# Gated cross-attention and quantized MLP on one core: probabilities turned by DMA instead of TensorE, weight jobs re-slotted, half of the gated magnitudes taken a stage earlier

## The chip, the cores and the metric

One core of one Trainium2 chip. The metric is device microseconds of one execution. In the text PE is TensorE, PEld its weight load, DVE VectorE, ACT ScalarE, POOL GpSimd, SP SyncE; "SPq" is SP's queue of DMA issues. SP computes nothing: it issues nearly all transfers, in program order, and a wait in it holds everything behind.

## What is computed

The input x is 4 batches of 1024 rows by 512; the context has 64 rows per batch. 16 heads of 64.

```python
x = x + tanh(g_xattn) * attention(layernorm(x), ctx)   # softmax over 64 keys, causal mask; @ w_o
x = x + tanh(g_ffn) * ffn(layernorm(x))
# ffn, with q() = fake quantization to 16 bits by the largest magnitude of the whole tensor:
up, gate = q(x @ deq(w_up).T), q(x @ deq(w_gate).T)     # 1536 columns
f = q(gate * round16(sigmoid(gate)))
out = q(f * up) @ deq(w_down).T
# deq(): 4-bit weights, a scale for every block of 32
```

Each q() needs a maximum over all 4096 rows before the first value can be quantized, which is why the program has stages with a hard border between them.

## The kernel before

Every product that matters is made of f16 parts, high and low: a = ah + al, b = bh + bl, and ah·bh + ah·bl + al·bh, three matmuls with 512 columns. Five stages follow each other, with a barrier of all engines at each border.

1. **Front** (`front_phase`): weights of attention are loaded and multiplied into per-batch matrices A (queries times keys) and V (values times w_o), then attention runs over 32 tiles of 128 rows, in steps. `schedule` calls on each engine a `step(b, k, ...)`; in step k the work of several tiles is done, each at another point of its life: layernorm of tile k+2, scores of tile k, softmax of tile k−1, values of tile k−2, second layernorm and output of tile k−3. The loop runs over eight steps, one batch (counted here as steps 3 to 10, and by k modulo 8).
   - PE, step k: 8 transposes (L1096) of the probabilities `pr` (f32, 128 by 1024) of tile k−2 into PSUM `pT`; 24 matmuls of scores (L1072); 24 of values (L1043). In steps 0 and 1 the next batch's A (`keys`, L1009) and V (`four_heads`, L1023) are made in between, and ACT and DVE split them in parts.
   - ACT and DVE split the turned probabilities from PSUM: `pTh` (L690), `pTl` (L906), in two halves each. DVE then subtracts the row maximum (L804, L808), ACT takes exp (L714), DVE sums (L839) and takes the reciprocal (L842), POOL multiplies (L652, `prob_done`).
   - SP, step k: stores x1 and x2, loads the next x, turns `nh`, `nl` of tile k+2 by DMA (L582).
   - **Jobs** (class `Jobs`): each dequantizes 128 by 512 of a weight: load, `job_scale` (DVE), `job_divide` (POOL), multiply back (DVE, `deq_done`), `hi` (ACT), `lo` (POOL or DVE), turn, store. In attention there are four a batch for w_gate, with two sets of buffers (`JB = 4`, NJ = 2), and SP turns them by DMA (L597).
2. **Gate** (`gate_phase`): 96 products of 12 matmuls (L1414), 24 in each round of its loop; ACT evicts (L1304), DVE takes extremes, SP spills to `gate_d`. Six jobs a round prepare w_up (first half, turned by DMA, L1246) and w_down (second half, turned by PE in `job_turn`, L334, and stored straight from `hi` and `lo`, L361).
3. **Up** (`up_phase`): 96 products. Beside it, for each of 32 tiles of 1536 columns, ACT takes the sigmoid of the gate (L1555); in the first half DVE searches the largest gated value (`lowest`), in the second (`slot_of(k)` gives tile k its product, k from 32) DVE computes f = gate · sigmoid · scale into `nq` as int16 (`gated`, L1603). A fresh product's maximum costs DVE one more operation (L1643).
4. **Magnitudes** (first half of `down_phase`): max |f · up| over everything. Per tile ACT makes |up| as integers (L1820) and |f| (L1826), DVE multiplies and reduces (L1850). For every third tile, `signed(k)`, ACT leaves |f| out and DVE makes two passes, with either sign. PE has nothing to do but `keep_warm`.
5. **Down**: quantize f · up (L1903), split it, 96 times 12 matmuls (L1937), `finish` adds x1, output.

The waits around the change, in the code's words:

```python
def signed(k):                                    # magnitudes, before
    return k == 0 or k % 3 == 2
if have(k - 2):                                   # PE's step, before
    pe.wait_ge(*tile(prob_done, b, j))
    ...
        mm = pe.transpose(pT[:, p * P:(p + 1) * P], pr[j % 2][:, p * P:(p + 1) * P], ident[:, :])
```

## Time and profile before

| | us |
|---|---|
| runs before: median (lowest to highest) | 1346.55 (1345.92 to 1348.36) |
| the profiled execution, its own time | 1344.37 |
| its span, first to last instruction | 1342.5 |
| front: first matmul of attention's scores / last of values, start | 50.7 / 481.8 |
| gate: first / last product matmul, start | 492.0 / 745.9 |
| up: first / last product matmul, start | 751.3 / 999.8 |
| magnitudes: first / last reduction, start | 1006.1 / 1083.7 |
| down: first product matmul, start | 1088.8 |

How to read what follows: a row of a timeline has the start, the length, the engine, the line of the kernel, the operation, what it writes and reads, how many instructions are merged, and in brackets how long the engine sat idle before and who released it. Matmuls are pipelined: one of 512 columns shows as 0.38 us, but the next starts 0.216 us later. A row of windows has the stretch, then for each engine its busy time and count, the granted clock of TensorE as a share of 2.4 GHz, the DMA engines' share and GB/s.

### The profile page before, as it was taken

The numbers are of one execution on the slowest core, as the hardware profiler recorded it, in microseconds if no ns is written. First come the engines' busy times: TensorE is split into PE (matmuls) and PEld (weight loads), VectorE is DVE, ScalarE is ACT, GpSimd is POOL, SyncE is SP. The second block draws the span as 40 slices with busy tenths as digits, with TensorE's granted clock in tenths as the row PEclk, the third lists the DMA queues.
The fourth block names the chain that finished last, engine by engine and source line by source line (L and its number), as shares of the span: only waits on it lengthen the run. The fifth ranks groups of instructions, "written<-read, shape, count | busy, mean of one in ns | idle before, by whom it ended". The sixth has DMA issues, their size and how long they took to land. (4 is left out here: it accounts for less than half of the span.)

```text
span 1342.5 us, 18904 instructions
## 1 busy us (share of the span) xinstructions
PE 1218.1 (91%) x5937; PEld 593.9 (44%) x5937; DVE 1001.7 (75%) x1444; ACT 672.2 (50%) x782; POOL 291.6 (22%) x375
## 2 busy tenths in 40 slices
PE   7899899999899989999999999999980079999998
PEld 6644544544444444444444444444430034444443
DVE  2778789779777667777777699979999975555554
ACT  3534444444353334444443588857669963343341
POOL 0246435535534221111111222300210000000000
PEclk9999999999999999999999999999995589999999
DMA  9123523533434458787876899943389854454453
GB/s 333 35 53 106 140 84 84 140 94 98 124 91 130 139 195 227 239 257 233 244 214 205 292 329 339 328 140 132 133 274 340 300 181 142 164 182 162 163 176 106
DMA packets 187403, 246.64 MB, mean 184 GB/s; under 512 B 99280, under 2 KB 111568, under 8 KB 187344
## 3 DMA queue, kind: packets, MB, share of 16 engines
q1 hardware_dynamic: 187056, 245.95, 57.0%
q8 instruction: 25, 0.41, 0.1%
q14 instruction: 34, 0.28, 0.1%
q10 hardware_dynamic: 288, 0.00, 0.0%
HBM read 136.32 MB, written 91.23 MB: 169 GB/s over the span
## 5 line engine op out<-in xcount | busy, mean ns | idle before, releaser
L1414 PE MATMUL gpG<-xph,Wh 128*128 128x512 f16 x384 | 145.6, 379 | 1.4 <-DVE xpl L1329 1.4
L1937 PE MATMUL pD<-Wh,xph 128*128 128x512 f16 x384 | 145.5, 379 | 1.0 <-DVE xpl L1912 1.0
L1414 PE MATMUL gpG<-xpl,Wh 128*128 128x512 f16 x384 | 145.5, 379 | 0.0
L1414 PE MATMUL gpG<-xph,Wl 128*128 128x512 f16 x384 | 145.5, 379 | 0.0
L1414 PE MATMUL pU<-xph,Wh 128*128 128x512 f16 x384 | 145.5, 379 | 0.0
L1414 PE MATMUL pU<-xpl,Wh 128*128 128x512 f16 x384 | 145.5, 379 | 0.0
L1414 PE MATMUL pU<-xph,Wl 128*128 128x512 f16 x384 | 145.5, 379 | 0.0
L1937 PE MATMUL pD<-Wl,xph 128*128 128x512 f16 x384 | 145.5, 379 | 0.0
L1937 PE MATMUL pD<-Wh,xpl 128*128 128x512 f16 x384 | 145.5, 379 | 0.0
L1304 ACT ACTIVATE gst<-gpG,rw 128x512 f32<-128x512 f32 x96 | 65.7, 685 | 130.9 <-PE gpG L1414 103.2
L1342 DVE TENSOR_REDUCE gmx<-gst 128x512 f32 (+1 forms) x96 | 65.4, 682 | 56.6 <-ACT gst L1304 56.4
L1072 PE MATMUL pS<-Ah,xh 128*128 128x512 f16 x256 | 76.2, 379 | 4.1 <-DVE Vl L783 4.1
L1555 ACT ACTIVATE gb<-nq,sc 128x1536 f32<-128x1536 int16 x48 | 75.3, 1568 | 4.6 <-POOL nq L1535 4.4
L1428 PE MATMUL pD<-ident 128*128 128x512 f16 x28 | 7.8, 440 | 75.6 <-DVE pmx L1850 75.6
L1072 PE MATMUL pS<-Ah,xl 128*128 128x512 f16 x256 | 76.1, 379 | 0.0
L1072 PE MATMUL pS<-Al,xh 128*128 128x512 f16 x256 | 76.1, 379 | 0.0
L652 POOL TENSOR_TENSOR pr<-pr,srec 128x1024 f32<-128x1024 f32 x32 | 60.8, 1901 | 68.2 <-DVE srec L842 67.8
L1569 ACT ACTIVATE ust<-pU,rw 128x512 f32<-128x512 f32 x72 | 49.0, 683 | 45.4 <-PE pU L1414 40.1
L690 ACT ACTIVATE pTh<-pT 128x512 f16<-128x512 f32 x64 | 34.7, 595 | 68.3 <-PE pT L1096 68.2
L714 ACT ACTIVATE pr<-pr,fit 128x1024 f32<-128x1024 f32 x32 | 36.7, 1148 | 62.9 <-DVE pr L808 44.1
L313 POOL TENSOR_TENSOR gjw<-gjw,gjinv 128x512 f32<-128x512 f32 x24 | 25.2, 1049 | 190.4 <-DVE gjinv L301 190.4
L1343 DVE TENSOR_REDUCE gmx<-gst 128x512 f32 (+1 forms) x96 | 64.8, 675 | 0.0
(248 smaller groups left out, 2615.5 us busy)
## 6 DMA issues: line engine op xcount, KB each, us to landing
dub<-up_d SPq DMA_DIRECT2D x42, 768.0 KB, 4.7
gate_d<-gst SPq DMA_DIRECT2D x96, 256.0 KB, 3.2
gb<-gate_d SPq DMA_DIRECT2D x24, 768.0 KB, 6.9
up_d<-ust SPq DMA_DIRECT2D x72, 256.0 KB, 5.0
eu<-up_d SPq DMA_DIRECT2D x22, 768.0 KB, 6.6
xr<-xn_d SPq DMA_DIRECT2D x9, 1024.0 KB, 6.4
xin<-in_x SPq DMA_DIRECT2D x32, 256.0 KB, 3.6
x_d<-x SPq DMA_DIRECT2D x32, 256.0 KB, 2.3
```

The lines of the kernel that those rows point to most:

```text
L313: pool.tensor_tensor(blocks(J.w[n][:, :]), blocks(J.w[n][:, :]), spread(J.inv[:, n, :]), ALU.mult).then_inc(J.div_done, 1)
L652: pool.tensor_tensor(p3, p3, srec[:, j % 2, :].unsqueeze(2).to_broadcast([P, HEADS, CK]), ALU.mult).then_inc(prob_done, 1)
L690: act.activation(pTh[:, cs], pT[:, cs], ACT.Copy, scale=P_TOP).then_inc(pTh_done, 1)
L714: act.activation(pr[j % 2][:, :], pr[j % 2][:, :], ACT.Exp, scale=S_UNIT).then_inc(exp_done, 1)
L1072: mm = pe.matmul(pS[k % 2][:, hf * 512:(hf + 1) * 512], xs[k % 4][:, cs], As[:, kt, hf * 512:(hf + 1) * 512], start=(kt == 0 and xs is xh ...
L1304: act.activation(stage[n][:, :], pG[m % 3][:, :], ACT.Copy, scale=row_scale[0][:, it:it + 1]).then_inc(g_sb, 1)
L1342: dve.tensor_reduce(gmx[:, 1, bass.ds(2 * IT * i + m, 1)], stage[m % NS][:, :], X, ALU.min).then_inc(g_neg, 1)
L1343: dve.tensor_reduce(gmx[:, 0, bass.ds(2 * IT * i + m, 1)], stage[m % NS][:, :], X, ALU.max).then_inc(g_pos, 1)
L1414: mm = pe.matmul(ps[:, :], Ws[:, it, kt * P:(kt + 1) * P], xs[:, kt, :], start=(kt == 0 and Ws is Wh and xs is xh), stop=(kt == KT - 1 and ...
L1555: act.activation(gb[k % NG][:, :], nq[:, k % QT, :], ACT.Sigmoid, scale=S_G).then_inc(sig_done, 1)
L1569: act.activation(stage[n][:, :], pU[m % NU][:, :], ACT.Copy, scale=scale[:, it:it + 1]).then_inc(u_sb, 1)
L1937: mm = pe.matmul(pD[4 * t + q][:, :], os_[n][:, cs], Ws[:, it, :], start=(it == 0 and os_ is oh and Ws is Wh), stop=(it == IT - 1 and os_ ...
```

## The change

- **Attention.** The probabilities are split before they are turned: ACT writes `p_high`, DVE `p_low`, each 128 by 1024 in one instruction, from SBUF. SP turns each in two halves by DMA (four DMA transposes a tile) into one of two buffers `pTh`, `pTl`. PE's transposes and PSUM's part in it are gone; PE multiplies the values of tile k−3 in step k, so second layernorm and output move to tile k−4, and there is one step more (k to BQ+3). V is made in step 2 instead of 1.
- **Jobs in attention** have four sets of buffers and one slot more to the end: `lo` moves behind POOL's probabilities and `job_divide`, `hi` to the start of ACT's step, `deq` behind DVE's sums.
- **Gate.** w_down's jobs are turned by DMA like w_up's; their stores come one job later, and the last one's waits at the end of the stage's queue for its turn.
- **Up, magnitudes, down.** For every second tile (`AWAY`), DVE's `gated` writes into a staging buffer `f_away`; ACT writes |f| into `nq`, SP spills f to `f_d`. Magnitudes need no |f| for these tiles; of the others every fourth is `signed`. Down loads f of these tiles again (`load_f`).

```diff
@@ front_phase, SP's step
+                if have(k - 2):
+                    j = k - 2
+                    sp.wait_ge(*tile(pl_done, b, j))
+                    sp.sem_inc(J.apart, 1)
+                    sp.wait_ge(*tile(o_ps, b, j - 2))
+                    sp.sem_inc(J.apart, 1)
+                    for part_, to in ((p_high, pTh), (p_low, pTl)):
+                        for cs in halves:
+                            sp.dma_start_transpose(blocks_of(to[j % 2][:, cs]), part_[:, cs]).then_inc(pt_in[j % 2], 16)
-                j = k - 3
+                j = k - 4
...
@@ front_phase, POOL's step (job_divide stays ahead of it)
-                    pool.tensor_tensor(J.lo[n][:, :], J.d[n][:, :], J.hi[n][:, :], ALU.subtract).then_inc(J.lo_done, 1)
...
+                    pool.tensor_tensor(J.lo[q][:, :], J.d[q][:, :], J.hi[q % 2][:, :], ALU.subtract).then_inc(J.lo_done, 1)
@@ front_phase, ACT's step
-                    act.wait_ge(*tile(o_ps, b, j - 1))
-                    for h, cs in enumerate(halves):
-                        act.wait_ge(*part(pT_ps, b, j, h))
-                        act.activation(pTh[:, cs], pT[:, cs], ACT.Copy, scale=P_TOP).then_inc(pTh_done, 1)
+                    act.wait_ge(*tile(prob_done, b, j))
+                    act.wait_ge(*p_turned(b, j - 1))
+                    act.activation(p_high[:, :], pr[j % 2][:, :], ACT.Copy, scale=P_TOP).then_inc(ph_done, 1)
@@ front_phase, DVE's step
+                        dve.wait_ge(*tile(ph_done, b, j))
+                        dve.scalar_tensor_tensor(out=p_low[:, :], in0=pr[j % 2][:, :], scalar=P_TOP, in1=p_high[:, :],
+                                                 op0=ALU.mult, op1=ALU.subtract).then_inc(pl_done, 1)
@@ front_phase, PE's values and step
-                j = k - 2
+                j = k - 3
                 if have(j):
+                    pe.wait_ge(*p_turned(b, j))
...
-                    for p in range(PAIRS):
-                        mm = pe.transpose(pT[:, p * P:(p + 1) * P], pr[j % 2][:, p * P:(p + 1) * P], ident[:, :])
@@ gate_phase, end of SP's round
+            turned_store(sp, i, JR - 1, job_dst(i, JR - 1))
@@ gate_phase, PE
-                        if it % 4 == 3 and t:
-                            job_turn(pe, J, i, 3 * t + it // 4, ident)
@@ up_phase
+        away = {(m // IT, m % IT): [k for k in range(QT, 2 * QT) if k - QT in AWAY and slot_of(k) + 3 == m] for m in range(FT * IT)}
...
+                    for k in away[j, it]:
+                        sp.wait_ge(f_done, k + 1)
+                        sp.dma_start(f_d[AWAY.index(k - QT), :, :], f_away).then_inc(f_out, 16)
...
+                    for k in away[j, it]:
+                        act.wait_ge(f_done, k + 1)
+                        act.activation(nq[:, k - QT, :], f_away, ACT.Abs).then_inc(f_abs, 1)
...
+                if k - QT in AWAY:
+                    to, n = f_away, AWAY.index(k - QT)
+                    if n:
+                        dve.wait_ge(f_abs, n)
+                        dve.wait_ge(f_out, 16 * n)
@@ down_phase
+            stay = [k for k, g in enumerate(ORDER) if g not in AWAY]
...
-                return k == 0 or k % 3 == 2
+                return k in stay and stay.index(k) % 4 == 0
```

Three places of the order of instructions. First SP's queue in one step of attention with a job's store and turn (k = 7 before, k = 9 of the change). `pTh`, `pTl` are the turned probabilities, `xh`, `xl` the turned layernorm, `pjhiT` the turned job, `x_d`, `xn_d` the outputs. Before:

```order
L558 DMA x_d<-x 128x512
L561 ISA
L561 DMA xin<-in_x 128x512
L563 DMA xn_d<-x 128x512
L577 REGISTER_ALU
L582 DMA_TRANSPOSE xh<-nh 128x4x128
L582 DMA_TRANSPOSE xl<-nl 128x4x128
L589 ISA
L589 DMA wgate_hi<-pjhiT 128x512
L589 DMA wgate_lo<-pjloT 128x512
L597 DMA_TRANSPOSE pjhiT<-pjhi 128x4x128
L597 DMA_TRANSPOSE pjloT<-pjlo 128x4x128
```

and of the change:

```order
L568 DMA_TRANSPOSE pTh<-p_high 128x4x128 x2
L568 DMA_TRANSPOSE pTl<-p_low 128x4x128 x2
L573 ISA
L573 DMA x_d<-x 128x512
L576 ISA
L576 DMA xin<-in_x 128x512
L578 DMA xn_d<-x 128x512
L592 REGISTER_ALU
L597 DMA_TRANSPOSE xh<-nh 128x4x128
L597 DMA_TRANSPOSE xl<-nl 128x4x128
L604 ISA
L604 DMA wgate_hi<-pjhiT 128x512
```

Four DMA transposes now stand at the head of each step's issues, ahead of the two of the layernorm and the job's two. Second, POOL in a step with a job's `lo`: `pjlo` is the job's low part, `pr` the probabilities, `pjw` the job's division, `nl` the low part of the next tile's layernorm. Before:

```order
L645 ISA [waits pj_hi]
L646 TENSOR_TENSOR pjlo<-pjd,pjhi 128x512 [waits pj_turn_in0]
L652 TENSOR_TENSOR pr<-pr,srec 128x1024 [waits rec]
L312 REGISTER_ALU
L313 TENSOR_TENSOR pjw<-pjw,pjinv 128x512 [waits pj_inv]
L317 TENSOR_SCALAR pjq<-pjw 128x512 [waits pj_div,pj_deq]
L661 TENSOR_TENSOR nl<-xn,nh 128x512 [waits xt_in1,xh]
```

and of the change:

```order
L661 TENSOR_TENSOR pr<-pr,srec 128x1024 [waits rec]
L315 REGISTER_ALU
L316 TENSOR_TENSOR pjw<-pjw,pjinv 128x512 [waits pj_inv]
L320 TENSOR_SCALAR pjq<-pjw 128x512 [waits pj_div,pj_deq]
L669 ISA [waits pj_hi]
L670 TENSOR_TENSOR pjlo<-pjd,pjhi 128x512 [waits pj_turn_in0]
L674 REGISTER_ALU [waits xh]
L675 TENSOR_TENSOR nl<-xn,nh 128x512 [waits xt_in0]
```

The job's `lo`, which waits for ACT and for a DMA transpose, has moved from ahead of the probabilities to behind them. Third, the end of SP's queue in the gate stage, of the change (before, the last rows are the two stores of `gjhi` and `gjlo` without the transposes ahead):

```order
L1201 DMA gate_d<-gst 128x512 x2
L1246 DMA wdown_hi<-gjhiT 128x4x128
L1246 DMA wdown_lo<-gjloT 128x4x128
L1235 DMA_TRANSPOSE gjhiT<-gjhi 128x4x128
L1235 DMA_TRANSPOSE gjloT<-gjlo 128x4x128
L1246 DMA wdown_hi<-gjhiT 128x4x128
L1246 DMA wdown_lo<-gjloT 128x4x128
L1151 UNCONDITIONAL_BRANCH
```

The last job is turned and then stored behind everything else, in front of the stage's border.

## Rows read from the trace of the kernel before

**Rows 1.** The page: span and share of each engine.
```profile
PE 1218.1 (91%) x5937; PEld 593.9 (44%) x5937; DVE 1001.7 (75%) x1444; ACT 672.2 (50%) x782; POOL 291.6 (22%) x375
```

**Rows 2.** Windows of attention: us, busy (x instructions) of five engines, clock, DMA, GB/s.
```profile
178.45:287.90 109.45, 102.76 (x548) 52.58 (x544) 87.81 (x149) 48.61 (x71) 52.78 (x77) 1.00 0.38 106
...
396.87:481.39 84.52, 80.51 (x402) 39.26 (x398) 58.80 (x87) 29.75 (x42) 30.25 (x48) 1.00 0.46 134
```

**Rows 3.** Timeline of PE in attention: start us, us, instruction, idle before it.
```profile
214.39 1.09 PE L1096 MATMUL pT<-ident,pr 128*128 128x128 f32 x8 [0.64 <-POOL pr L652]
215.32 0.59 PE L1072 MATMUL pS<-Ah,xh 128*128 128x512 f16 x2
...
220.50 0.38 PE L1043 MATMUL pX<-Vh,pTh 128*128 128x512 f16 x1
...
253.51 1.09 PE L1096 MATMUL pT<-ident,pr 128*128 128x128 f32 x8 [2.74 <-POOL pr L652]
...
272.18 1.04 PE L1096 MATMUL pT<-ident,pr 128*128 128x128 f32 x8
...
461.36 0.59 PE L1072 MATMUL pS<-Ah,xl 128*128 128x512 f16 x2
...
481.82 0.38 PE L1043 MATMUL pX<-Vh,pTl 128*128 128x512 f16 x1
```

**Rows 4.** Timeline of DVE, one step of attention with a job.
```profile
215.95 0.68 DVE L846 TENSOR_REDUCE xmx<-x 128x1 f32<-128x512 f32 x1
...
224.83 0.63 DVE L283 TENSOR_REDUCE pjmx<-pjw 128x16 f32<-128x512 f32 x1
...
227.58 0.67 DVE L846 TENSOR_REDUCE xmx<-x 128x1 f32<-128x512 f32 x1
```

**Rows 5.** Groups by line, POOL and ACT in attention: busy, mean ns, idle before.
```profile
L652 POOL TENSOR_TENSOR pr<-pr,srec 128x1024 f32<-128x1024 f32 x32 | 60.8, 1901 | 68.2 <-DVE srec L842 67.8
...
L661 POOL TENSOR_TENSOR nl<-xn,nh 128x512 f16<-128x512 f32 x32 | 37.0, 1157 | 23.4 <-ACT nh L678 23.4
...
L690 ACT ACTIVATE pTh<-pT 128x512 f16<-128x512 f32 x64 | 34.7, 595 | 68.3 <-PE pT L1096 68.2 <-issue 0.2
```

**Rows 6.** One line of SP's queue (min/median/max ns), and its landing.
```profile
L582 SPq DMA_TRANSPOSE xl<-nl x32: 1239/1253/2307, 40.5 to 446.6; - x32
...
DMA to landing us min/median/max: 2.4/2.5/4.2
```

**Rows 7.** Timeline at one gate job's turn, and at the gate's end.
```profile
533.88 0.60 PE L334 MATMUL gjbank<-ident,gjd 128*128 128x128 f32 x4
534.31 0.38 PE L1414 MATMUL gpG<-xph,Wh 128*128 128x512 f16 x1
...
749.13 0.51 SPq L361 DMA_DIRECT2D wdown_lo<-gjlo  x1
...
750.59 0.40 PE L1421 MATMUL upR<-ident,sc 128*128 128x128 f32 x2 [1.52 <-PEq L1157]
```

**Rows 8.** The up stage's second half: a window, DVE's gating, landing of a store.
```profile
905.00:930.00 25.00, 25.00 (x117) 11.37 (x116) 25.00 (x23) 16.50 (x17) 2.26 (x2) 1.00 0.43 148
...
L1603 DVE SCALAR_TENSOR_TENSOR nq<-nq,sc,mb x16: 1802/1811/2971, 897.9 to 998.4; 128x1536 int16<-128x1536 int16 x16
...
up_d<-ust SPq DMA_DIRECT2D x72, 256.0 KB, 5.0
```

**Rows 9.** The magnitude stage: timeline at its start, in it and at its end; a window.
```profile
1006.07 1.82 DVE L1850 CUSTOM_DVE_ANT_0 xfa<-nq,dui,pmx 128x1536 int16<-128x1536 int16 x1 [0.22 <-DVE nq L1695]
...
1022.83 1.48 ACT L1826 ACTIVATE last_m<-nq 128x1536 int16<-128x1536 int16 x1
...
1030.21 1.48 ACT L1826 ACTIVATE xfa<-nq 128x1536 int16<-128x1536 int16 x1
...
1010.00:1020.00 10.00, 0.00 (x0) 0.00 (x0) 9.74 (x11) 8.73 (x7) 0.00 (x0) 0.50 0.97 377
...
1085.43 0.08 DVE L1850 DVE_READ_ACCUMULATOR2_ANT pmx<- 128x1 f32 x1
```

More of the change, by code:

```diff
@@ L402, in front_phase @@
         pr = [sb(ph, f"pr{n}", [P, INNER], F32) for n in range(2)]
-        pTh = sb(ph, "pTh", [P, INNER], F16)
-        pTl = sb(ph, "pTl", [P, INNER], F16)
+        p_high = sb(ph, "p_high", [P, INNER], F16)
+        p_low = sb(ph, "p_low", [P, INNER], F16)
         x1 = [sb(ph, f"x1{n}", [P, H], F32) for n in range(2)]
@@ L438, in front_phase @@
         Vl = sb(ph, "Vl", [P, PAIRS, H], F16)
+        pTh = [sb(ph, f"pTh{n}", [P, INNER], F16) for n in range(2)]
+        pTl = [sb(ph, f"pTl{n}", [P, INNER], F16) for n in range(2)]
         pw = [pS[0][:, 0:512], pS[0][:, 512:1024]]
@@ L452, in front_phase @@
                o_ps x1 stats2 mean2 eps2 rstd2 x2 x2max""".split())
-        pT_ps, pTh_done, pTl_done = (sem(n, 16) for n in ("pT_ps", "pTh", "pTl"))
+        ph_done, pl_done = (sem(n, 8) for n in ("ph", "pl"))
+        pt_in = [sem(f"pt_in{n}", 64) for n in range(2)]
         kbd_set, vb_set = sem("kbd_set"), sem("vb_set")
@@ L465, in schedule @@
         def schedule(eng, step, straight=False):
-            for k in range(-2, 3):
+            for k in range(-2, 4):
                 step(0, k, lambda j: j >= 0, False)
@@ L470, in schedule @@
                 for b in range(B - 1):
-                    for k in range(3, BQ + 3):
+                    for k in range(4, BQ + 4):
                         step(b, k, lambda j: True, True)
@@ L708, in step @@
                     normal(b, j, xn, xin[j % BQ], mv, rs, xn_done)
+                q = job_at(k, jobs, 2)
+                if q is not None:
+                    act.wait_ge(*at(J.deq_done, JB * b, q + 1))
+                    act.wait_ge(*at(turn_in[q % 2], 16 * JB * b, 32 * (q // 2)))
+                    act.activation(J.hi[q % 2][:, :], J.d[q][:, :], ACT.Copy).then_inc(J.hi_done, 1)
                 def exponentials():
@@ L972, in step @@
                     fit_v()
[L973 to L974 removed]
+                if have(k - 4):
+                    largest(b, k - 4)
             for r in range(2):
@@ L1048, in values @@
                     if which == 0 and p < PAIRS - 1:
-                        if p == 2 and have(j):
-                            pe.wait_ge(*part(pTl_done, b, j, 1))
                         keys(b, k, ahead, p + 1)
@@ L1166, in gate_phase @@
         AHEAD = 5
-        J = Jobs(mk, ph, "gj", JR, NJ, [pb(ph, "gjbank")])
-        turned = [[sb(ph, f"gj{part}T{n}", [P, 512], F16) for part in ("hi", "lo")] for n in range(3)]
-        turn_in = [sem(f"gj_turn_in{n}", 32) for n in range(3)]
+        J = Jobs(mk, ph, "gj", JR, NJ, None)
+        turned = [[sb(ph, f"gj{part}T{n}", [P, 512], F16) for part in ("hi", "lo")] for n in range(JR)]
+        turn_in = [sem(f"gj_turn_in{n}", 32) for n in range(JR)]
         pG = [pb(ph, f"gpG{n}") for n in range(3)]
@@ L1784, in _, with load_f @@
                     sp.dma_start(xub[k % NB], up_d[g, :, :]).then_inc(xu_in[k % NB], 16)
+                def load_f(g):
+                    n = AWAY.index(g)
+                    if n < 2:
+                        sp.wait_ge(xui_done, [k for k in range(QT) if k % NB == 2 + n][-1] + 1)
+                    else:
+                        sp.wait_ge(o_done, AWAY[n - 2] + 4)
+                    sp.dma_start(fr[n % 2], f_d[n, :, :]).then_inc(fr_in[n % 2], 16)
+                sp.wait_ge(f_out, 16 * len(AWAY))
+                for g in AWAY[0:2]:
+                    load_f(g)
                 for g in range(2):
```

235 lines of the change are left out of this document (115 added, 120 removed).

## The prediction

> **What bounds the kernel now.** I read the page first: PE is busy for 91% of the span and DVE for 75% [rows 1], so the question is where PE is not the limit. The stages answer it. Gate, up and down are 1152 matmuls each at a pitch of 0.216 us, 248.8 us, and by the table they take hardly more. Two places are left. **Attention**: the windows over whole batches [rows 2] show 109.45 us a batch with PE busy 102.8, DVE 87.8. In PE's timeline [rows 3] a step starts with the eight transposes, and what PE waits for there is POOL's multiplication `pr` (0.64, 2.74 us). **Magnitudes**: 1006.1 to 1085.5 us, PE idle, DVE and ACT both near full, DMA share up to 0.97 [rows 9]. A gain must come from these, or from work taken off PE.
>
> **Attention, PE's side.** The transposes cost 0.93 us a step (214.39 to 215.32), scores 5.18, values again 5.18 (24 at 0.216) [rows 3]. A plain step needs 11.3 us before, 10.4 after. The step with A takes 18.67 us (253.51 to 272.18), the next, with V, 15.72 (to 287.90, end of the window): after, 17.7 and 14.8. A batch of the change is then 6 x 10.36 + 17.7 + 14.8 = 94.7 us of PE, 14.7 less than it takes now. That is the floor, if everyone else keeps up.
>
> **Attention, the others.** DVE's step with a job is 11.63 us without a gap (215.95 to 227.58), 2.75 of it the job's scale (from 224.83) [rows 4]. DVE's new `low` is one instruction of 1024 instead of two of 512, about 1.2 us as now. Over a batch I get 94.7 for DVE too: step 4 about 11.0, three of 11.63, steps 0 and 2 about 14.5, three plain ones of 9.9. In a plain step the circle is reciprocal, POOL 1.90, ACT's `p_high` 1.1 (two of 0.595 [rows 5], less overlap), `low`, subtraction, exp, sums: 9.9 us, under PE's.
> The new resource is SP's queue. A DMA transpose is issued for 1.25 us and lands 2.5 after its start [rows 6], so four take 4.9 us and 1.3 more to land. ACT may write `p_high` again only when they have landed. This closes a chain over two steps: `nl` done, two transposes of it (2.5), next step's four (6.2), `p_high` 1.1, `low` 1.2, DVE up to the reciprocal 5.6 (its step [rows 4] without job, `low` and first statistics), POOL's `pr` 1.9 and `nl` 1.2 [rows 5], with waits between 20.1 us, 10.0 a step. Without jobs PE stays the bound, barely. With jobs the chain of the even steps takes in 7.8 us of SP (two turns of 2.5, stores, loads), 6.1 of POOL (division and `lo`, operations of `nl`'s size, now ahead of `nl`), 1.2 of DVE and some 7 of parts of A and V: 80.2 + 22.1 = 102.3 us a batch. That is above both floors. I take 102.5; bounds 95 (the floor) and 109.5 (no idle gained).
>
> Terms, attention:
> - three batches at 102.5 instead of 109.3: -20.4;
> - the last batch's four plain steps and scores, 52.3 us now (409.55 to 461.8), 4 x 10.36 + 5.18 = 46.6 after: -5.7;
> - the start: the values of the first tile leave step 2, so step 3 starts 0.93 + 5.18 earlier: -6.1, paid back at
> - the end: the last scores to the last values take 461.8 to 482.0, 20.2 us [rows 3]. Of the change: subtraction 2.5, then `p_high` of the last tile must wait until the tile before has landed (its `low` at 4.4, 6.2 to land: 10.6), 1.1, 1.2, 6.2, values 5.2 = 24.3: +4.1.
> Sum -28.1, bounds from -51 (94.9 a batch) to -8 (109).
>
> **Gate.** A turn of four transposes costs 0.43 us (533.88 to 534.31) [rows 7], 12 of them 5.2 us. But the stage ends by SP: its last issue ends at 749.64, and all engines go on at 750.5 [rows 7]. Now the last job is turned first: two issues 2.5 and a landing 1.3 more, 3.8 us. Net -1.4 (bounds -5.2, +1).
>
> **Up.** DVE is busy 25.00 of 25 us in the second half [rows 8]: it has no room. ACT gets 16 magnitudes of 1.48 us over 106 us and has 8.5 of 25 free, so it carries them. The staging buffer is one: tile n+2 may be gated when f of tile n is in memory, and SP issues that three products after its slot. Slots of such tiles are 2 or 3 products (2.59 us each) apart. The first time DVE is ready at about 903.5 us and the spill lands at 906.7 (issue 902.7; landing 2 to 5, the latter the row of the smaller spill [rows 8]); later DVE's lag hides it. A full DVE can't win the lag back: +2.5 (bounds 0, +12, twice 16 waits of 0.4).
>
> **Magnitudes.** Now 43 passes in 79.4 us, 1.85 each; ACT's five operations per three tiles take 7.38 us (1022.83 to 1030.21), 1.48 each, so the two engines are equally full [rows 9]. After: DVE 32 + 4 = 36 passes, ACT 32 + 12 = 44 operations: 36 x 1.83 = 65.9 and 44 x 1.48 = 65.1 us: -13.4. A tile is 768 KB every 2.06 us, 382 GB/s; the window at 0.97 share shows 377 [rows 9]. Six buffers and four early loads cover most of it: +1 (bounds 0, +5). `keep_warm` starts a shorter time ahead: +0.4. Sum -12.0.
>
> **Down** gets 16 loads of 384 KB, issued a tile ahead, under PE's 245 us: 0. Nothing else moves there.
>
> **Sum**: -28.1 - 1.4 + 2.5 - 12.0 = -39.0. The profiled execution took 1344.4 us (span 1342.5 and 1.9 around it), so 1305.4 on it; the median of the runs is 2.2 above, and 1346.6 - 39 = **1307.6 us**, 2.9% less.
>
> **Rivals.**
> - *PE's floor is reached* (SP runs ahead where steps 0 and 2 are long, and DVE's lag is elastic by most of a step): 94.9 a batch, 23 us less than forecast: 1285. For it: both floors are equal, and only the chain through SP is longer; its extras may overlap better than I add them. Against: two engines at their floor at once is rare. 0.17.
> - *VectorE and GpSimd get in each other's way*, or the chain through SP is longer: 107.5 a batch: +15, with +3 in up: 1325. For it: DVE's gating shows 2971 ns beside a median of 1811 [rows 8], with POOL at work then; `low` now reads both operands from SBUF, and POOL's `nl` or division may run beside it. Against: `nl` mostly ends where `low` starts. By the Trainium skill (GPSIMD Engine Reference, 1. Specifications) the two share their SBUF interfaces when DVE has two SBUF inputs; this case's slow instance agrees. 0.23.
> - *SP's queue becomes the bound, slower than before.* A transposing DMA of the six to eight in a row takes longer than 1.25 us: the row has one at 2307 ns, and a landing of 4.2 [rows 6]. SP's step is six transposes and 1.0 of plain issues, in four steps a batch two transposes and 1.3 more. At 1.2 us each that is 83 us a batch; at 1.8, 8 x 11.8 + 4 x 4.9 = 114; three batches +14, last batch +2, end +6, less 11 from the rest: 1358. It decides from 1.7 us a transpose. Against: 64 issues of this kind in this attention keep to the median, though never more than four in a row. 0.05.
>   The Trainium skill (VectorE: DVE Perf Modes, The three transpose paths and Rules for kernel authors) says to turn 128 by 128 on TensorE if PSUM will do, 390 ns against 1309 by DMA. As an estimate by that page, 16 blocks a tile would be 21 us of DMA a step if they ran one by one, twice PE's step. The row disagrees: four blocks are issued in 1.25 us and there in 2.5.
> - *Only magnitudes gain*: the probabilities' turn is late in every step (a wait of PE on `pt_in` takes the place of the one on POOL): 109 a batch, 1327 to 1340. 0.05; the rest is scattered.
>
> **Chances.** Forecast 0.50 (1297 to 1316), floor 0.17, contention 0.23, queue 0.05, late turn 0.05. The range from **1285 to 1330** leaves out the queue, half of the late turn and the lower part of the floor. A change of 0.2%, 2.7 us, is about what can be told from none. Faster 0.94, within 0.01, slower 0.05.
>
> **What would show it.** Attention: PE's L1072 to L1052 without transposes; a batch 102.5 us; PE's wait on a landing of `pTh`/`pTl` in the step with A, ACT's `p_high` waiting for a DMA in steps 7 to 3, not in plain ones; transposes at 1.2 us each. Last scores to last values 24 us. Gate: products 248.8 without gap, barrier 3 us after the last product is reduced. Up: one wait of DVE on the spill at the first tiles, end 2 to 3 us later. Magnitudes 66 us, DMA share above 0.95. Wrong: a batch under 97 or over 107, DVE waiting for the spill again and again, ACT waiting for loads in magnitudes.

## The result, and the profile after

The changed kernel takes **1363.84 us** (median of 4 runs, 1362.95 to 1365.2), the kernel before in the same session 1346.24 (1344.47 to 1348.36): ratio 1.0131, 95% interval 1.0113 to 1.0149. It is 1.3% slower; 1307.6 was forecast, 1285 to 1330. The profiled execution took 1362.95 us, span 1361.1, 18.6 above the span before. The page's head and its row of the clock:

```profile
span 1361.1 us, 18490 instructions
PE 1206.1 (89%) x5633; PEld 568.2 (42%) x5633; DVE 992.9 (73%) x1398; ACT 674.9 (50%) x757; POOL 307.9 (23%) x375
...
PEclk9979899899899989999999899999996579999999
```

PE has 12 us less to do than before [rows 1], so the loss is waiting. Two bounds of its terms were broken as well: a batch had 109.5 us as its upper bound ("no idle gained") and took up to 113.3, and the gate had +1 and got +7.8. The stages, cut at PE's instructions in both timelines (us, after minus before):

| stretch | before | after | difference | forecast |
|---|---|---|---|---|
| to the first batch's scores of tile 3 (the first behind V in the change, the second before) | 82.60 | 80.94 | -1.7 | -6.1 |
| three batches | 327.8 | 335.0 | +7.2 | -20.4 |
| last batch, to the end of its last scores | 51.4 | 48.3 | -3.1 | -5.7 |
| last scores to last values | 20.2 | 33.2 | +13.0 | +4.1 |
| gate, from the last values to the first product of up | 269.2 | 277.0 | +7.8 | -1.4 |
| products of up | 248.9 | 251.0 | +2.1 | 0 |
| last product of up to the turn of its maximum | 2.1 | 9.3 | +7.1 | +2.5 |
| from there to the first product of down | 86.5 | 72.7 | -13.8 | -12.0 |
| rest | 253.7 | 253.7 | 0 | 0 |

**Attention.** PE's timeline around the step with A of the second batch, and the scores behind V at the two ends of that batch (start, us, engine, line, operation, what it waited for):

```profile
189.83 0.60 PE L1078 MATMUL pS<-Ah,xh 128*128 128x512 f16 x2 [2.23 <-DVE Vl L796]
...
239.62 0.39 PE L1052 MATMUL pO<-Vh,pTh 128*128 128x512 f16 x1 [0.76 <-DMA pTl<-p_low]
...
254.18 2.07 PE L1019 MATMUL pS<-kbd,wqT 128*128 128x128 f32 x8 [9.21 <-DMA pTl<-p_low]
256.04 0.63 PE L1052 MATMUL pX<-Vh,pTh 128*128 128x512 f16 x1
...
302.60 0.61 PE L1078 MATMUL pS<-Ah,xh 128*128 128x512 f16 x2 [2.23 <-DVE Vl L796]
```

The batch takes 302.60 - 189.83 = 112.8 us (the three: 108.9, 112.8, 113.3), while plain steps take the 10.36 forecast. Most of what is lost stands in one place: at the step with A, where values come first in the step, PE waits 9.21 us for the tile's low part to land (5.96 and 8.21 in the other batches). Who waits in attention, by the waits of PE, ACT and SP (60 to 500 us):

```profile
PE pS L1019 <- DMA pTl<-p_low: 23.4, 3, 9.2
PE pS L1078 <- DVE Vl L796: 9.0, 4, 2.3
PE pO L1052 <- DMA pTl<-p_low: 7.5, 3, 6.0
...
ACT p_high L703 <- DMA pTl<-p_low: 55.7, 19, 5.5
...
SPq L593 <- POOL nl L675: 52.5, 23, 9.9
...
SPq L563 <- DVE p_low L917: 10.1, 4, 3.9
```

A row of waits has the total in us, the number of times and the longest. The last two rows are the telling ones: SP waits for `p_low` four times only. It stands at the wait for `nl` (23 times, 52.5 us), in front of the probabilities' turns of the next step. One step with a job on GpSimd and on SP's queue:

```profile
236.16 2.23 POOL L661 TENSOR_TENSOR pr<-pr,srec 128x1024 f32<-128x1024 f32 x1
238.79 1.05 POOL L316 TENSOR_TENSOR pjw<-pjw,pjinv 128x512 f32<-128x512 f32 x1 [0.40 <-DVE pjinv L290]
...
241.76 2.13 POOL L675 TENSOR_TENSOR nl<-xn,nh 128x512 f16<-128x512 f32 x1
```

```profile
244.06 1.21 SPq L597 DMA_TRANSPOSE xh<-nh  x1
245.31 1.25 SPq L597 DMA_TRANSPOSE xl<-nl  x1
246.90 0.35 SPq L250 DMA_DIRECT2D pjw<-in_L_ffn_w_gate  x1
247.50 2.50 SPq L568 DMA_TRANSPOSE pTh<-p_high  x2
250.06 2.57 SPq L568 DMA_TRANSPOSE pTl<-p_low  x2
```

And VectorE in the same step, which has no gap of more than 0.17 us in it:

```profile
235.82 0.25 DVE L854 RECIPROCAL srec<-ssum 128x16 f32<-128x16 f32 x1
...
237.26 1.16 DVE L288 TENSOR_SCALAR pjs<-pjmx 128x16 f32<-128x16 f32 x1
...
241.55 1.33 DVE L917 SCALAR_TENSOR_TENSOR p_low<-pr,p_high 128x1024 f16<-128x1024 f32 x1
```

`p_low` ended at 242.88; its turns started at 247.50 and the last landed at 253.9. VectorE's step is long too: from one `p_low` to the next 12.30 us (229.25 to 241.55), where a step with a job took 11.63 before [rows 4] and PE now needs 10.36. One part of that is `L288`, an operation on 16 columns, 1.16 us here and 0.32 at 225.50 in the timeline of before; in the mean of attention's 12 it takes 1267 ns, 842 before. Not every step is like this one: in the four steps with jobs of this batch VectorE takes 50.3 us from `p_low` to `p_low` (204.71 to 255.04), in the other four, with A and V among them, 62.5 (191.23 to 204.71 and 255.04 to 304.01):

```profile
191.23 1.19 DVE L917 SCALAR_TENSOR_TENSOR p_low<-pr,p_high 128x1024 f16<-128x1024 f32 x1
...
204.71 1.23 DVE L917 SCALAR_TENSOR_TENSOR p_low<-pr,p_high 128x1024 f16<-128x1024 f32 x1 [4.28 <-ACT p_high L703]
...
255.04 2.10 DVE L917 SCALAR_TENSOR_TENSOR p_low<-pr,p_high 128x1024 f16<-128x1024 f32 x1 [0.55 <-ACT p_high L703]
...
304.01 1.19 DVE L917 SCALAR_TENSOR_TENSOR p_low<-pr,p_high 128x1024 f16<-128x1024 f32 x1
```

**The end of attention, and the stages behind.** PE's timeline at the last values, at the end of gate, of up and of magnitudes:

```profile
471.97 0.39 PE L1052 MATMUL pX<-Vh,pTh 128*128 128x512 f16 x1 [2.39 <-DMA pTl<-p_low]
...
483.28 0.61 PE L1052 MATMUL pO<-Vh,pTh 128*128 128x512 f16 x1 [5.95 <-DMA pTl<-p_low]
...
492.19 0.39 PE L1052 MATMUL pX<-Vh,pTh 128*128 128x512 f16 x1 [0.98 <-DMA pTl<-p_low]
...
507.66 0.61 PE L1405 MATMUL gpG<-xph,Wh 128*128 128x512 f16 x1 [0.89 <-DVE xpl L1324]
...
764.43 2.75 PE L1419 MATMUL gpX<-ident 128*128 128x512 f16 x12
773.09 0.66 PE L1412 MATMUL upR<-ident,sc 128*128 128x128 f32 x2 [5.91 <-PEq L1151]
...
1034.68 0.48 PE L1412 MATMUL upR<-ident,sc 128*128 128x128 f32 x1 [9.26 <-DVE sc L1661]
...
1097.24 7.28 PE L1419 MATMUL pD<-ident 128*128 128x512 f16 x20 [62.09 <-DVE pmx L1881]
```

At 1097.24 is the gain: PE waits 62.09 us for VectorE's 36 passes of 1.81 us, 75.6 before for 43. At 1034.68 is what it cost: up ends with VectorE 9.26 us behind (2.1 before), since it waited for the spill of `f`, five times and not once. ScalarE's wait for a spill of gate's products more than doubled. The same waits before, then of the change:

```profile
PE pD L1428 <- DVE pmx L1850: 75.6, 1, 75.6
...
ACT gst L1304 <- DMA gate_d<-gst: 24.7, 10, 3.5
...
PE upR L1421 <- DVE sc L1651: 2.1, 1, 2.1
```

```profile
DVE x_rows L1613 <- DMA f_d<-x_rows: 9.7, 5, 3.0
...
ACT gst L1304 <- DMA gate_d<-gst: 58.3, 15, 6.7
```

### The profile page after: what moved, and what is told of

The parts are those of the page before. It is cut to its first block and busy times, and to the rows that moved or that the text cites. A ratio compares the mean times of both kernels' runs of the same rounds, so it can differ in the third digit from the quotient of the medians.

```text
span 1361.1 us, 18490 instructions
## 1 busy us (share of the span) xinstructions
PE 1206.1 (89%) x5633; PEld 568.2 (42%) x5633; DVE 992.9 (73%) x1398; ACT 674.9 (50%) x757; POOL 307.9 (23%) x375
## 5 line engine op out<-in xcount | busy, mean ns | idle before, releaser
L1078 PE MATMUL pS<-Ah,xh 128*128 128x512 f16 x256 | 77.6, 385 | 13.9 <-DVE Vl L796 9.0
L661 POOL TENSOR_TENSOR pr<-pr,srec 128x1024 f32<-128x1024 f32 x32 | 63.8, 1993 | 78.1 <-DVE srec L854 77.3
L703 ACT ACTIVATE p_high<-pr 128x1024 f16<-128x1024 f32 x32 | 33.8, 1055 | 70.6 <-DMA pTl<-p_low 55.7
L917 DVE SCALAR_TENSOR_TENSOR p_low<-pr,p_high 128x1024 f16<-128x1024 f32 x32 | 42.3, 1323 | 36.1 <-ACT p_high L703 35.9
L686 ACT ACTIVATE xn<-xin,rs 128x512 f32<-128x512 f32 x32 | 26.0, 812 | 83.0 <-POOL rs L649 83.0
```

Of the source, the lines that this page charges most:

```text
L661: pool.tensor_tensor(p3, p3, srec[:, j % 2, :].unsqueeze(2).to_broadcast([P, HEADS, CK]), ALU.mult).then_inc(prob_done, 1)
L686: act.activation(to[n][:, :], src[:, :], ACT.Identity, bias=rs_[:, n, 2:3], scale=rs_[:, n, 1:2]).then_inc(done, 1)
L703: act.activation(p_high[:, :], pr[j % 2][:, :], ACT.Copy, scale=P_TOP).then_inc(ph_done, 1)
L917: dve.scalar_tensor_tensor(out=p_low[:, :], in0=pr[j % 2][:, :], scalar=P_TOP, in1=p_high[:, :], op0=ALU.mult, op1=ALU.subtract).then_inc( ...
L1078: mm = pe.matmul(pS[k % 2][:, hf * 512:(hf + 1) * 512], xs[k % 4][:, cs], As[:, kt, hf * 512:(hf + 1) * 512], start=(kt == 0 and xs is xh ...
```

## The experiments

Each time is a median, with the ratio to the kernel before on the same chip and its interval. A batch runs from the scores behind V to those of the next. The kernel before has medians from 1346.1 to 1349.0 us in these sessions, so differences between two experiments are given from their traces where a few us matter.

### The three parts alone

**only_attention**: of the diff only what stands in `front_phase` and the jobs' class.

> The kernel before with the change's attention alone (probabilities turned by DMA, values a step later, jobs reordered); gate, up, magnitudes and down are those of before. By the prediction on record attention gives 28.1 us: 1318. By the trace of the whole change attention lost 15.5 us (last values end at 497.4 us and not at 482.0) and nothing behind it belongs to it: 1362, the last values again near 497. A rival: the gate and up lose time because attention leaves DMA or the clock in another state; then this kernel comes out slower than 1364, with a gate of more than 254 us.

1363.05 us, 1.0099 (1.0075 to 1.0123). Batches 109.2, 112.6, 113.3; the last values end at 500.5 (482.0 before, 497.4 in the whole change). The same waits, 23.0 us of them in the three steps with A. Up takes 248.9, and 5.0 us pass from gate's last product to up. Theory held: the attention part alone loses in its batches what the whole does (335.1 us for the three, 335.0 there), 1.7 us more behind them (83.2 us to the last values and not 81.5), and nothing of gate's end.

**only_gate**: of the diff only what stands in `gate_phase`.

> The kernel before with the change's gate alone (w_down's weights turned by DMA, the last store behind the last turn). Prediction on record: -1.4, 1345. Theory from the trace: products 256.4 us and not 253.8 in spite of 12 turns less, of which 2.4 is the first products at the low clock, and 10.2 and not 5.4 us from the last product to the first of up, then 2.2 us of up's first products at 1.2 GHz since PE idled 5.9 us: if these belong to the gate, +7 to +9.6: 1353 to 1356. Rival: the slow first products follow PE's idle time at the end of attention, not the gate: then the products of the gate take about 254, and the sum is +5 to +7.

1353.98 us, 1.0043 (1.0023 to 1.0063). Products from 493.65 to 749.18, 255.5 and not 253.8, with 12 turns less: ScalarE's waits for a spill hold PE up by 3.4. Behind the longest of these waits the granted clock fell too: 0.73 from 640 to 645, 12 matmuls where 23 fit at the full clock. Then 10.5 us to up's first product (5.4 before), and 1.1 more in up. These three are 7.9 us in the trace; the ratio says 5.8. The first products run at the full clock here (granted 1.00 from 493.6 to 499.0, against 0.50 from 507.6 to 512.4 in the whole change): the rival was right in that, those belong to attention's idle end. The barrier, and the slower spills, are gate's own. With 7.9 in the trace and 5.8 by the ratio the run doesn't decide between the theory's sum (+7 to +9.6) and the rival's (+5 to +7).

**only_magnitudes**: of the diff only what stands in `up_phase` and `down_phase`.

> The kernel before with the early magnitudes alone (up, magnitudes, down of the change). Prediction on record: +2.5 in up, -12.0 in magnitudes: 1336.7. Theory from the trace: -13.8 from the first wide reduction to the first product of down, +7.2 between up's last product and the turn of its maximum (DVE's five waits of 9.7 us in all for the spill of f, in an engine without room): 1339.6. Rival: those waits are longer in the whole change only because other DMA work is late; then DVE is done 2 to 3 us after up's last product, as before, and the kernel takes 1333.

1340.83 us, 0.9958 (0.994 to 0.9976). PE's two waits, at the end of up and of magnitudes:

```profile
PE pD L1431 <- DVE pmx L1893: 62.1, 1, 62.1
PE upR L1424 <- DVE sc L1673: 11.6, 1, 11.6
```

The rival fell: VectorE's waits for the spill are there without the other parts (11.8 us, 5 times). From the turn of up's maximum to the first product of down it wins 14.8 us (86.5 before, 71.7 here), and 9.4 are given back in up. The three ratios multiplied give 1.0099 x 1.0043 x 0.9958 = 1.0100, against 1.0131. With intervals of 0.2% on each, this difference of 0.3% can't be told from none.

### What the staging buffer costs

**only_magnitudes_two**: a second buffer for `f`. It lies where the fourth of down's early loads would go; that load is issued behind the last spill instead.

```diff
-        f_out, f_abs = sem("u_f_out"), sem("u_f_abs")
+        f_out, f_abs = [sem(f"u_f_out{n}") for n in range(2)], sem("u_f_abs")
+        f_away = [f_away, early_u[3][:, 0:I // 2].bitcast(I16)]
...
-                    to, n = f_away, AWAY.index(k - QT)
-                    if n:
-                        dve.wait_ge(f_abs, n)
-                        dve.wait_ge(f_out, 16 * n)
+                    n = AWAY.index(k - QT)
+                    to = f_away[n % 2]
+                    if n > 1:
+                        dve.wait_ge(f_abs, n - 1)
+                        dve.wait_ge(f_out[n % 2], 16 * (n // 2))
```

> only_magnitudes with two staging buffers for f (the second in the fourth of down's early loads, which comes after the last spill instead), so that VectorE waits for the spill before the last. Theory (the 11.8 us of VectorE's waits on the one buffer, in an engine without room, are the 9.4 us that up ends later): the waits go, up's maximum is turned 2 to 4 us after its last product and not 11.6, magnitudes stay at 62 us: 1331 to 1334, from 1340.8. Rival: the end is late because ScalarE's 16 extra magnitudes (1.48 us each) or VectorE's slower gating (2.42 us in some) fill the engine: then 1337 to 1341. Rival: the fourth load is now late at the start of magnitudes: +1 to +3 us there.

1335.1 us, 0.9921 (0.9904 to 0.9937). No wait of VectorE on a spill is left, and PE waits 3.18 us for up's maximum, not 11.57; in magnitudes it still waits 62.8 us. The theory held: the loss in up was the one buffer, not the extra magnitudes on ScalarE.

### SP's queue, the landing, or VectorE

**nl_before_jobs**: GpSimd's `nl` moved up, right behind `pr`.

```diff
+                if have(k + 2):
+                    ...
+                    pool.tensor_tensor(nl[j % 2][:, :], xn[j % 2][:, :], nh[j % 2][:, :], ALU.subtract).then_inc(xl_done, 1)
                 q = job_at(k, jobs, 0)
                 if q is not None:
                     job_divide(pool, J, b, q, q + 1)
                 q = job_at(k, jobs, 2)
...
-                if have(k + 2):
-                    ...
-                    pool.tensor_tensor(nl[j % 2][:, :], xn[j % 2][:, :], nh[j % 2][:, :], ALU.subtract).then_inc(xl_done, 1)
```

> The whole change, with GpSimd's nl (x's low part) moved ahead of the job's division and low part, right behind pr. Theory A (SP's queue is the chain: it stands at the wait for nl while p_low has long been done; p's four turns start 1.7 to 6.1 us after p_low, at 219.8, 233.2, 247.5, 262.4, 279.8 us): nl ends some 3 us earlier in the steps with jobs, p's turns too, and the wait of 9.2 us in the step with A falls to 2 to 5 us: 4 to 7 us a batch, 1345 to 1352. Theory B (VectorE is the chain: its step with a job takes 12.3 us against PE's 10.36, and it is without a gap from 214 to 247 us): nothing but the place of the wait changes, within 3 us of 1363.8. Rival C: ACT's and VectorE's part of the job comes later and the next step with them: slower by some us.

1356.43 us, 1.0058 (1.0037 to 1.0079). SP's wait for `nl` falls from 52.5 to 36.7 us. Batches 106.5, 111.5, 110.7, so 2.4, 1.3 and 2.6 less; PE's waits in the step with A 1.65, 6.84 and 6.83. Less than theory A said and more than B: SP's wait is a part of the chain, and behind it VectorE is full (its `p_low` at 215.14, 227.94, 240.57, 253.25, without a gap of more than 0.23 us between).

**plain_p_turns**: the four turns of the probabilities become plain copies. It leaves out the turning, so PE multiplies other data; only its time is of use.

```diff
-                            sp.dma_start_transpose(blocks_of(to[j % 2][:, cs]), part_[:, cs]).then_inc(pt_in[j % 2], 16)
+                            sp.dma_start(to[j % 2][:, cs], part_[:, cs]).then_inc(pt_in[j % 2], 16)
```

> The whole change, with the four turning DMAs of a tile's probabilities replaced by four plain copies of the same 128 KB (the probabilities then stand unturned, so the values are those of other data). A plain issue takes SP 0.35 to 0.6 us and not 1.27, so 2.7 to 3.7 us of SP and part of the landing go from every step. Theory A (chain through SP and the landing): the 9.2 us wait of PE in the step with A falls under 3 us, a batch to 104 or less, the end of attention by some 8 us more: 1325 to 1335. Theory B (VectorE's step of 12.3 us with a job): PE's wait stays at 6 us or more, a batch at 109 to 110, only the end gains: 1345 to 1352. Rival: the turns hold up other engines' DMA and SBUF traffic; then VectorE's own instructions get shorter.

1352.38 us, 1.004 (1.0023 to 1.0058). Batches 109.2, 112.0, 111.0, waits in the step with A 3.69, 6.46 and 5.97; the end of attention gains more. SP's issues of the low part, of the whole change and then here (min/median/max ns):

```profile
L568 SPq DMA_TRANSPOSE pTl<-p_low x64: 1188/1267/2040, 71.9 to 489.6; - x64
```

```profile
L568 SPq DMA_DIRECT2D pTl<-p_low x64: 477/601/815, 69.4 to 478.9; - x64
```

That is close to theory B's forecast (1345 to 1352, batches 109 to 110): with half of the turns' issue gone from SP (1.13 and 1.25 us for what took 2.50 and 2.57) the three waits in the steps with A fall by 7.3 us, but the three batches by 2.8 only. The chain passes through SP but is not made of it.

**nl_narrow_max**: on top of nl_before_jobs 0.6 us less of VectorE a step.

```diff
-                dve.tensor_reduce(xmx[:, bass.ds(BQ * b + j, 1)], x2[j % 2][:, :], X, ALU.max,
+                dve.tensor_reduce(xmx[:, bass.ds(BQ * b + j, 1)], x2[j % 2][:, 0:32], X, ALU.max,
```

> nl_before_jobs, and VectorE takes the maximum of x2 over 32 of the 512 columns only (0.1 and not 0.68 us a tile), so the scale of x is that of a part. In nl_before_jobs PE still waits 6.84 us in the step with A and 2.24 before. Theory B (VectorE, with jobs 12.7 us a step, is what is left): its step gets 0.55 us shorter, four to five steps before the wait, so PE's waits fall by 2 to 3 us a batch: 1348 to 1351. Theory A (SP's chain): nothing, 1356.

1349.06 us, 1.0013 (0.9996 to 1.003): 7.4 less than nl_before_jobs. Batches 104.4, 109.2, 108.5, each 2.1 to 2.3 us shorter. The size is theory B's, the place isn't: PE's waits in the step with A stay (1.00, 6.83 and 6.84 us). In the second batch 1.1 us came from the scores' wait for VectorE's `pr` (2.24, then 1.14) and 1.1 from the keys and values of the step with A, which VectorE's `Al` holds up (17.49 us to the scores, then 16.36).

**two_p_and_nl**: on top of nl_before_jobs two buffers for `p_high` and for `p_low`.

```diff
-                    act.wait_ge(*p_turned(b, j - 1))
-                    act.activation(p_high[:, :], pr[j % 2][:, :], ACT.Copy, scale=P_TOP).then_inc(ph_done, 1)
+                    act.wait_ge(*p_turned(b, j - 2))
+                    act.activation(p_high[j % 2], pr[j % 2][:, :], ACT.Copy, scale=P_TOP).then_inc(ph_done, 1)
```

> nl_before_jobs, with two buffers each for p_high and p_low (the second pair lies where up's late stages do), so that ScalarE's p_high waits for the landing of the tile before the last. Theory A: ScalarE's waits for the landing (55.7 us of them in the whole change) were part of the chain; they go, PE's wait in the step with A falls to 2 us or less, the end of attention gains 5 us: 1335 to 1345. Theory B: with nl early VectorE has no gap in the steps with jobs, p_high comes earlier but p_low doesn't; only the last tiles gain, 3 to 6 us: 1350 to 1353.

1344.24 us, 0.9983 (0.997 to 0.9996). PE's waits, the first two rows, and ScalarE's for `p_high`, where no landing is left:

```profile
PE pS L1019 <- DMA pTl<-late_st: 11.3, 3, 5.4
PE pS L1078 <- DVE Vl L796: 9.0, 4, 2.3
...
ACT p_high L703 <- POOL pr L661: 28.5, 16, 3.1
```

Batches 106.5, 107.9, 107.6, and the last stretch of attention 4 us shorter: 10.4 us in the trace up to the last values, 12.2 by the medians. The time is theory A's, the waits of 4.1 and 5.4 us that stay are more than it allowed (2). So there were three causes: `nl` behind the jobs, one buffer held until it has landed, and VectorE's step. Each was taken away on top of the ones before; what each is worth alone, or in another order, was not tried.

### Two engines in each other's way

**scale_late**: on top of two_p_and_nl, the job's scale changes places with the maximum of `x2`.

```diff
-                q = job_at(k, jobs, 0)
-                if q is not None:
-                    job_scale(dve, J, b, q, unit[:, 3 * q + b:3 * q + b + 1])
                 if k == 0:
                     fit_v()
                 if have(k - 4):
                     largest(b, k - 4)
+                q = job_at(k, jobs, 0)
+                if q is not None:
+                    job_scale(dve, J, b, q, unit[:, 3 * q + b:3 * q + b + 1])
```

> two_p_and_nl, with VectorE's scale of the job one instruction later, behind the maximum of x2 (0.68 us). In the whole change the scale's tensor_scalar over 16 columns takes 1267 ns in the mean (842 in the kernel before; 0.18 where GpSimd stands still), always while GpSimd multiplies pr (1.99 us, from 0.1 us behind the reciprocal). Theory C (the two engines get in each other's way there, and VectorE's step with a job is the bound): it falls to 0.3 to 0.7 us, the step to 12 us or less, PE's wait in the step with A by some 2 us in each batch: 1338 to 1341, from 1344.2. Rival: nl now stands behind pr and gets in the way instead: the instruction stays above 1 us, 1344. Rival: the integers of the job come late and GpSimd's chain with them: 1346 or more.

1343.87 us, 0.9984 (0.9974 to 0.9994). VectorE's groups in attention, first of the whole change, then here (busy us, mean ns | idle before):

```profile
L288 DVE TENSOR_SCALAR pjs<-pjmx 128x16 f32<-128x16 f32 x12 | 15.2, 1267 | 0.4
```

```profile
L288 DVE TENSOR_SCALAR pjs<-pjmx 128x16 f32<-128x16 f32 x12 | 8.3, 693 | 0.4
```

The instruction falls by 0.57 us as theory C said, but the time doesn't follow. Where it went shows at the maximum of `x2`, of two_p_and_nl and then here:

```profile
L858 DVE TENSOR_REDUCE xmx<-x 128x1 f32<-128x512 f32 x31 | 20.8, 669 | 9.1 <-ACT x L686 9.1
```

```profile
L858 DVE TENSOR_REDUCE xmx<-x 128x1 f32<-128x512 f32 x31 | 21.0, 677 | 17.9 <-ACT x L686 17.9
```

The maximum now comes earlier and waits for ScalarE's `x2`: 17.9 us in attention and not 9.1. VectorE is 11.8 us less busy (6.9 in `L288`, 3.8 in `L278` behind it, 1.1 in `p_low`), and 8.8 of it came back as this wait. In some steps the engines still meet: a `p_low` takes 1.92 us (235.89) beside GpSimd's `pjlo`, and that step is 12.69 us (223.20 to 235.89). What is left is 0.5 us a batch. Theory C had the instruction right and the path wrong: ScalarE stood next in line.

This is what the Trainium skill says in SBUF — State Buffer (SBUF: two separate sides), on the port pair that VectorE and GpSimd share: whoever starts first holds it for its whole instruction, against VectorE's instructions in a fast mode or with two inputs in SBUF. The trace agrees. In the whole change `L288` starts at 237.26, inside GpSimd's `pr` (236.16, 2.23 us), and ends at 238.42, 0.03 us behind it; `p_low`, with two inputs from SBUF, takes 2.10 us where it starts inside `nl` (255.04, 254.90) and 1.19 at its least.

### The clock

**warm_in_A**: PE works through its wait.

```diff
                 if have(j):
-                    pe.wait_ge(*p_turned(b, j))
                     pe.wait_ge(*tile(x1_done, b, j - 2))
+                    if which == 0:
+                        keep_warm(pe, pOut[j % 2][:, :], ident, 24)
+                    pe.wait_ge(*p_turned(b, j))
```

> The whole change, with 24 matmuls that are thrown away (5.2 us) on PE ahead of its wait for pTl in the step with A, into the bank that the values then start. The granted clock stood at 0.63 in PE's wait of 9.2 us (248.0 to 254.1) and at 0.51 in the 5.9 us behind it, with products of 634 ns and not 379: by the rows some 2.7 us of the step with A. Theory (the clock falls since PE idles): the granted clock stays at 1.00, the step with A is 2.5 to 3 us shorter in three batches, 1355 to 1357. Rival: the wait is over before the filler is (first batch 5.96 us): then up to nothing in that batch. Rival: the clock doesn't follow PE's idling: nothing, 1364, or some us more.

1365.93 us, 1.0128 (1.0099 to 1.0157), no gain. The windows over the wait and over the first part of the step with A, of the whole change and of this kernel (stretch, its length, busy us of PE, PEld, DVE, ACT, POOL, granted clock, DMA share, GB/s):

```profile
248.00:254.10 6.10, 0.00 (x0) 0.00 (x0) 5.40 (x13) 1.16 (x3) 4.43 (x5) 0.63 0.61 146
254.10:260.00 5.90, 5.82 (x22) 4.53 (x23) 5.03 (x8) 2.28 (x3) 2.60 (x4) 0.51 0.52 156
```

```profile
247.00:253.40 6.40, 3.62 (x17) 1.47 (x15) 5.71 (x13) 1.48 (x3) 4.63 (x6) 1.00 0.60 143
253.40:259.30 5.90, 5.85 (x31) 4.82 (x32) 5.04 (x8) 2.25 (x3) 2.60 (x4) 0.71 0.60 156
```

The clock does follow PE's idling: granted 1.00 in the wait and not 0.63, then 0.71 and not 0.51 (2.83 us of idle time were left). But from the first key to the scores it is 15.56 us here and 15.55 there. PE is done with keys and values 1.1 us sooner, and waits that much longer for VectorE's last part of A ahead of the scores (1.34 us for `Al` and not 0.26). The low clock cost nothing here, where PE was not the limit; a stretch with the clock at 1.00 throughout was not tried.

### The best version

**best**: attention of scale_late, gate of before, magnitudes with two buffers.

> Attention of scale_late, the gate of the kernel before, magnitudes with two staging buffers. By the sum of the parts: attention with nl early and two buffers ends near 481 us and with the late scale near 476 (before: 482.0); gate as before (the change's cost 5 to 9 us); up and magnitudes -12 to -14: 1326 to 1332, 1.1 to 1.5% under before. Rival: the parts do not add (the DMA queue at the end of attention, the clock at the start of the gate): 1333 to 1340.

**1330.36 us**, 0.9886 (0.9869 to 0.9902): 1.1% faster than before, 2.5% than the change. The last values end at 479.1 (482.0 before). By the parts one would get 13.9 us (11.0 of only_magnitudes_two, 2.9 in attention) and has 15.8 by the medians: inside the expected 1326 to 1332.

**best_narrow_max**: the narrow maximum on top of best, which leaves out most of that maximum.

> best, and VectorE takes the maximum of x2 over 32 of 512 columns (the scale of x is that of a part): 0.6 us less of VectorE in each of attention's steps, nothing else. In best a batch takes 106.0, 107.4 and 107.05 us against PE's floor, with PE's waits of 2.1, 6.4 and 4.3 us for pTl in the step with A. Theory B (with nl early and two buffers, what is left of the loss is VectorE's step of 12.3 to 12.7 us with a job against PE's 10.36): these waits fall by about 2 us each (four steps of 0.55), 1323 to 1326. Rival A (SP's turns and their landing are what is left): PE's waits and the time stay, 1330.

1321.08 us, 0.9803 (0.9782 to 0.9823). PE's waits in the steps with A fall to 8.8 us in all from 12.8, batches to 104.2, 105.1 and 104.8 (in best 106.0, 107.4 and 107.0). The waits fall by less than the 2 us a step with A of theory B, the time by more, 9.3 us: VectorE is a large part of what is left in attention.

## Why the prediction was wrong, point by point

- **Magnitudes, right**: -12.0 forecast, -13.8 measured. First to last reduction take 63.7 us (1038.59 to 1102.32) and not 66; `keep_warm`, forecast at +0.4, makes VectorE wait 2.09 us for PE behind the last one, 0.42 before. **Down, right**: 0.
- **Plain steps, right**: 10.36 us, the turns gone from PE. The gain on PE was real and went nowhere, except in the last batch.
- **The batch is where it failed.** "Over a batch I get 94.7 for DVE too" and "the chain of the even steps ... 102.3". Measured 112.8 in the second batch. Against PE's floor of 94.7 stand 3.0 us in the step with A (20.7 with its scores and not 17.7), 2.5 in the step with V (2.23 of it a wait for `Vl` ahead of the scores), 11.8 us of waits for landings, and about 0.8 of smaller ones; I had 7.8 for all.
- **The term that failed is "some 7 of parts of A and V"**, for which I had no row. My chain gives the four steps with jobs 2 x 20.1 + 15.1 = 55.3 us and the other four 2 x 20.1 + 7 = 47.2. Measured from `p_low` to `p_low` are 50.3 and 62.5. So the links with jobs were no longer than I had them, and the 7 us were 22.3. It could have been seen beforehand: PE's own floor for those four steps is 17.7 + 14.8 + 2 x 10.36 = 53.2, more than my chain had. Behind it stands a wrong overlap: I took the longest of three sums over a batch, as if an engine that is early in one step could lend its time to the next. In the steps with jobs VectorE and the chain need 12.6 us and PE 10.36; four times that difference is 8.9 us, and PE's wait ahead of A is 9.21. Then PE's long steps begin. That the sums fail in this way is worked out from the timelines; no run tests it by itself.
- **VectorE's step with a job** was 11.63 us in my working and is 12.2 to 13.5. My row held a job's scale of 0.32 us; in the same trace one that starts inside GpSimd's `pr` takes 1.44 (212.93). I took the lucky one, and the reordering puts all twelve there (1.16 to 1.44 us). The *chain through SP* I had named, with division and `lo` ahead of `nl`; a queue that issues in order stood 52.5 us at `nl`. On top of each other, nl_before_jobs gave 2.1 us a batch, two_p_and_nl 2.2, and nl_narrow_max prices VectorE at 2.1. My list of VectorE's steps has nine for a batch of eight: 94.7 is right with two plain ones.
- **Where values stand in the step with A.** Everywhere else the scores (5.18 us) come first and cover a late landing. With A they come last. I named this wait, and had 7.8 for the batch.
- **The start**: the first scores behind V came 1.7 us earlier and not 6.1. Values did leave step 2, but V's part there waits for VectorE: 2.63, 0.66 and 2.32 us.
- **The end, +13.0 and not +4.1.** I let the last tile's maximum and subtraction start at the end of the last scores. It starts at 472.40, 8 us later, since VectorE runs a step behind PE. From there each tile costs 9 us in series (`p_high` 473.95, then 483.32; values at 483.28, then 492.19): split, four turns, landing, only then the next `p_high`.
- **Gate, +7.8 and not -1.4.** SP's end, forecast +3.8, is +4.4 (PE waits 5.91 us at the border, 1.52 before). The turns' 5.2 us were eaten: transposing DMAs stand ahead of the spills in SP's order, and a late spill stops ScalarE and then PE (3.6 us); 2.4 us are first products at half the clock (granted 0.50 from 507.6 to 512.4) behind attention's idle end. In up another 2.1 are lost to the clock, after 5.9 us in which PE idled at the barrier.
- **Up, +7.1 at its end and not +2.5.** The bounds (0 to +12) held it, the value didn't. "later DVE's lag hides it" was the failing step: the lag grew by each wait, and the spill lands 5.0 us after its issue in the median, up to 6.4.
- **The rivals.** *Contention* (0.23) named two real mechanisms, but its price, 107.5 a batch, was a batch of the repaired kernel (107.9 in two_p_and_nl). That was luck. *SP's queue* (0.05) gave nearly the measured time, 1358, for another reason: the 128 turns took 1.23 and 1.27 us in the median, 2.04 at the most, not 1.7. *Only magnitudes gain* (0.05) had PE waiting for the turned probabilities in every step, 109 a batch; it waits for them mostly at the step with A.
  The Trainium skill's rule (VectorE: DVE Perf Modes, Rules for kernel authors), to turn on TensorE where PSUM will do, came out on the right side for the change as it stands; in best, attention turned by DMA ends at 479.1 us against 482.0. The page's figure of 1309 ns for one block by DMA (The three transpose paths) is not what decided: four blocks are issued in 1.27 us and there in 2.5, as the row had said.

What stays open: the order of gate's spills and turns on SP was not varied, so the 3.6 us are read from the trace, not tested. What makes the step with A 3.0 us longer in itself was not varied either, nor the order in which the three causes in attention are taken away. That a low clock costs 2 us at the start of gate and up is read from the trace as well.

## What to carry to other kernels

When work moves from a busy engine to a queue, don't ask only what the queue has to issue, but at which wait it will stand when the new work becomes ready, and who is late there: a queue in order is as late as the latest engine it waits for. Compute the new floor of every engine from the trace of its busiest kind of step, with a margin for what newly runs beside it, and add the longest engine step by step: a sum over a batch hides that four steps in a row run late and that their lag ends in one wait. A single buffer that is released by a landing (2.5 us and more) is a link of the chain; a second one was worth 10.4 us of attention's trace, and 5.7 us by the medians in up, for 4 KB and 3 KB a partition that lay idle in that stage.
